# Graph attention and experts on one core: queries from one f32 product in place of three bf16 ones

## The reference, cut to what matters

```python
def _L0_gnn_ref(node_features, edge_index, edge_relations, query_emb, Wq, bq, Wk, ...):
    enh = node_features + 0.1 * query_emb[None, :]
    Q = (enh @ Wq + bq).reshape(N, H, D)
    K = (enh @ Wk + bk).reshape(N, H, D)
    V = (enh @ Wv + bv).reshape(N, H, D)
    src, dst = (edge_index[0], edge_index[1])
    rel = rel_w[edge_relations]
    mod_k = K[src] + 0.2 * rel[:, None, :]
    scores = jnp.einsum('ehd,ehd->eh', Q[dst], mod_k) / D ** 0.5
    seg_max = jax.ops.segment_max(scores, dst, num_segments=N)
    ex = jnp.exp(scores - seg_max[dst])
    denom = jax.ops.segment_sum(ex, dst, num_segments=N)
    w = ex / denom[dst]
    agg = jax.ops.segment_sum(w[:, :, None] * V[src], dst, num_segments=N)
    ...
x = x + _L0_gnn_ref(_layernorm(x), ...)
x = x + _L0_ffn_ref(_layernorm(x)[None], ...)[0]
```

## Time and profile before

| what | us |
|---|---|
| median of three runs | 1356.09 (1348.56 to 1357.88) |
| the profiled execution's own time | 1346.19 |
| its span, first to last instruction | 1344.4 |

### The profile page before, as it was taken

The page is one execution under the profiler, slowest core; times in us unless marked ns, Lnnn a source line. Parts: engine busy times, 40 slices in busy tenths (PEclk is TensorE's granted clock), DMA queues, the critical chain, the costliest instruction groups (busy, mean ns, idle before and its releaser), DMA issues.

```text
span 1344.4 us, 23897 instructions
## 1 busy us (share of the span) xinstructions
PE 1080.3 (80%) x7032; PEld 851.6 (63%) x7033; DVE 894.0 (66%) x1856; ACT 666.2 (50%) x2365; POOL 716.4 (53%) x714
## 2 busy tenths in 40 slices
PE   8978567776767777676677777799599999999997
PEld 3445345555545555555555565567389999999996
DVE  4767767677777877777777768889944444444443
ACT  5532356667667776576676766557511111111111
POOL 4455555555555655555556554756055555445663
PEclk9997777778888978777878878897699999999999
DMA  6266666656766666567666665602744444655332
GB/s 211 94 180 189 195 196 192 202 183 178 221 189 206 193 194 204 179 202 210 198 199 198 174 208 142 202 5 92 256 119 118 100 100 95 184 150 130 53 52 28
DMA packets 112993, 215.77 MB, mean 160 GB/s; under 512 B 19403, under 2 KB 57211, under 8 KB 112891
## 3 DMA queue, kind: packets, MB, share of 16 engines
q0 software_dynamic: 47488, 132.68, 36.7%
q1 hardware_dynamic: 59973, 80.16, 18.4%
q10 hardware_dynamic: 5430, 1.73, 0.6%
HBM read 191.96 MB, written 22.54 MB: 160 GB/s over the span
## 4 chain that ended last, share of the span: by engine, by line
PE 49%; DVE 21%; issue 16%; another core or an unknown queue 9%; ACT 2%; DMA 1%; DVEq 1%; SPq 0%; POOL 0%; POOLq 0%
PE qe_ps L1920 13%; PE bank L1929 8%; PE qe_ps L1732 6%; DVE ring L881 6%; PE bank L1772 5%; PE bank L1920 4%; DVE acc L893 3%; PE qe_ps L1772 2%; DVE ring L875 2%; DVE score L887 2%; PE qe_ps L1837 1%; PE qe_ps L1650 1%; PE qe_ps L1909 1%; PE bank L1650 1%
## 5 line engine op out<-in xcount | busy, mean ns | idle before, releaser
L632 POOL DMA_INDIRECT ring<-kv_table,src_idx x440 | 421.0, 957 | 330.4 <-DVE ring L881 181.5
L1502 ACT ACTIVATE wv<-ring,wgt 128x64 f32<-128x64 f32 x1628 | 407.3, 338 | 52.9 <-remote 46.5
L1732 PE MATMUL qe_ps<-q,hot_t 128*128 x1320 | 237.1, 316 | 140.0 <-issue 87.6
L1732 PEld LDWEIGHTS qe_ps<-q,hot_t 128*128 128x128 bf16 x1320 | 134.6, 110 | 209.0 <-issue 179.3
L1772 PE MATMUL bank<-wv,hotf 128*128 128x260 f32 x588 | 188.6, 451 | 25.2 <-issue 18.8
L697 POOL DMA_INDIRECT out<-room,slot_i x64 | 119.2, 1863 | 154.9 <-DMA out<-room,slot_i 81.4
L1920 PEld LDWEIGHTS qe_ps<-xg_t,ring 128*128 128x128 f32 x1536 | 181.4, 192 | 4.9 <-issue 1.7
L1621 ACT ACTIVATE act<-qe_ps 128x512 f32<-128x512 f32 x64 | 38.2, 597 | 294.7 <-PE bank L1920 140.9
L875 DVE TENSOR_TENSOR ring<-ring,bank 128x1024 f32<-128x1024 f32 x110 | 133.3, 1212 | 75.8 <-remote 63.3
L1920 PE MATMUL qe_ps<-xg_t,ring 128*128 128x128 f32 x1536 | 182.0, 275 | 1.3 <-issue 0.7
L881 DVE TENSOR_TENSOR ring<-ring,qe_ps 128x512 f32<-128x512 f32 x220 | 148.8, 677 | 26.1 <-remote 18.2
(11 more groups left out here) (339 smaller groups left out, 1504.5 us busy)
## 6 DMA issues: line engine op xcount, KB each, us to landing
ring<-in_w SPq DMA_DIRECT2D x48, 512.0 KB, 7.1
t_row<-t_rows SPq DMA_DIRECT2D x55, 256.0 KB
d_row<-d_rows SPq DMA_DIRECT2D x55, 256.0 KB
ring<-kv_table,src_idx POOLq DMA_INDIRECT x440
kv_table<-ring SPq DMA_DIRECT2D x25, 256.0 KB, 2.0
out<-acc SPq DMA_DIRECT2D x26, 128.0 KB, 1.7
x_table<-ring SPq DMA_DIRECT2D x26, 128.0 KB, 1.9
ring<-in_x SPq DMA_DIRECT2D x12, 256.0 KB, 9.0
```

The costliest lines, as they stand in the source:

```text
L632: pool.indirect_dma_start(ring[:, u, place(g) * D:(place(g) + 2) * D], None, kv_table, bass.IndirectOffsetOnAxis(ap=src_idx[:, 4 * g + u:4 ...
L1502: ins = act.activation(wv[:, g % WV_N, u, h, 0:HD], v_rows(g)[:, u, h * HD:(h + 1) * HD], ACT.Copy, scale=w[:, col:col + 1])
L1732: ins = pe.matmul(q_ps[p % AHEAD][:, u * D:(u + 1) * D], hot_t[:, p // 4 % HB_N, hot_cols(p, u)], tile_of(q3, q_tiles[p % 4])[:, k * D:(k ...
```

## The change

Q stays in one f32 tensor `q_all`, copied from PSUM by ACT alone (`keep_q`). The one-hots are f32, six octs of them instead of seven. `queries` does one f32 product per step instead of three bf16 ones. `turn_hot` reads the high halves of the f32 one-hots as bf16. The pieces of Q go, with their semaphores. The tensors that lay over `q3` for the stage behind get their own space (`later`), and x lies over `q_all`. The copy `first` is made one oct earlier.

```diff
-HB_N = 7
+HB_N = 6
-        q3 = sb("q3", [P, NODE_TILES, 3 * D], BF16)
+        q_all = sb("q_all", [P, NODE_TILES, D])
+        later = sb("later", [P, KC * D + 2 * D + KC * NX + NX])
...
-        hot_t = eb("hot_t", [P, HB_N, 8 * P], BF16)
+        hot_t = eb("hot_t", [P, HB_N, 8 * P])
...
-            def rest_of_q(t):
-            def low_piece(t):
-            def pieces_of_q(first, end):
-            def pieces_beside(p):
-            pieces_of_q(0, Q_FIRST)
...
                 if rows_due:
                     factor_rows(rows_due)
-                    v.tensor_copy(first[:, :], hot_t[:, rows_due * CS // 8 % HB_N, 0:1])
+                if maxima_due:
+                    v.tensor_copy(first[:, :], hot_t[:, maxima_due * CS // 8 % HB_N, 0:1])
...
-            def high_piece(t):
+            def keep_q(t):
                 s_q.wait(act, t)
-                act.activation(q3[:, t, 0:D], q_bank(t), ACT.Copy).then_inc(s_high.sem, 1)
-            def middle_piece(t):
-                s_rest.wait(act, t)
-                act.activation(q3[:, t, D:2 * D], rest[:, t % 3, :], ACT.Copy).then_inc(s_mid.sem, 1)
+                act.activation(q_all[:, t, :], q_bank(t), ACT.Copy).then_inc(s_qk.sem, 1)
...
             def project_q(t):
-                s_rest.wait(pe, t - 3)
+                s_qk.wait(pe, t - 3)
...
-                s_lo.wait(pe, min(p, NODE_TILES - 1))
+                s_qk.wait(pe, min(p, NODE_TILES - 1))
                 for u in range(2):
-                    for k in range(3):
-                        ins = pe.matmul(q_ps[p % AHEAD][:, u * D:(u + 1) * D], hot_t[:, p // 4 % HB_N, hot_cols(p, u)], tile_of(q3, q_tiles[p % 4])[:, k * D:(k + 1) * D],
-                                        start=(k == 0), stop=(k == 2))
+                    ins = pe.matmul(q_ps[p % AHEAD][:, u * D:(u + 1) * D], hot_t[:, p // 4 % HB_N, hot_cols(p, u)], tile_of(q_all, q_tiles[p % 4]), start=True, stop=True)
...
-                    ins = pe.transpose(turn_ps.bitcast(BF16)[:, u * P:(u + 1) * P], hot_t[:, o % HB_N, u * P:(u + 1) * P], identb[:, :])
+                    ins = pe.transpose(turn_ps.bitcast(BF16)[:, u * P:(u + 1) * P], hot_t[:, o % HB_N, u * P:(u + 1) * P].bitcast(BF16)[:, 1::2], identb[:, :])
```

More of the change, by code:

```diff
@@ L301, in build @@
         assert at[0] <= NT * H * HB
-        q3_flat = q3[:, :, :].rearrange("p t c -> p (t c)").bitcast(F32)
+        x_again = q_all[:, :, :].rearrange("p t c -> p (t c)")
+        xre = q_all[:, :, :]
         at[0] = 0
[L306 to L313, removed]
+        w_o = carve(later, KC * D).rearrange("p (k n) -> p k n", k=KC)
+        gamma = carve(later, D)
+        beta = carve(later, D)
+        gate_w = carve(later, KC * NX).rearrange("p (k n) -> p k n", k=KC)
+        gate_b = carve(later, NX)
         w_expert = flat[:, 0:WB * WX].rearrange("p (b n) -> p b n", b=WB)
@@ L351, in build @@
         xn_st = late[:, 8 * P:8 * P + 2 * D].rearrange("p (b c) -> p b c", b=2)
-        at[0] = 3 * 4 * P
-        hot_flat = hot_t[:, :, :].rearrange("p m c -> p (m c)").bitcast(F32)
+        at[0] = 3 * 8 * P
+        hot_flat = hot_t[:, :, :].rearrange("p m c -> p (m c)")
         dval = carve(hot_flat, STEPS)
@@ L357, in build @@
         typ = carve(hot_flat, STEPS // 2, BF16)
-        assert at[0] <= HB_N * 4 * P
+        assert at[0] <= HB_N * 8 * P
         dst_t = late[0:PP, 0:4 * P].rearrange("p (q c) -> p q c", q=4)
@@ L371, in build @@
         w_q = [a[:, :, :].rearrange("p i c -> p (i c)") for a in (ends2, wgt)]
-        rest = carve(wv_flat, 3 * D).rearrange("p (s n) -> p s n", s=3)
         dif3 = carve(wv_flat, 3 * NT).rearrange("p (i t) -> p i t", i=3)
@@ L457, in build @@
         s_xn, s_xt, s_enh, s_mm, s_ev, s_kv = (Count(sem(n)) for n in ("s_xn", "s_xt", "s_enh", "s_mm", "s_ev", "s_kv"))
-        s_q, s_high, s_rest, s_mid, s_lo = (Count(sem(n)) for n in ("s_q", "s_high", "s_rest", "s_mid", "s_lo"))
+        s_q, s_qk = (Count(sem(n)) for n in ("s_q", "s_qk"))
         s_kst = [sem(f"s_kst{i}") for i in range(NS)]
@@ L741, in _ @@
                 row_scales(i)
-            def rest_of_q(t):
-                s_high.wait(v, t)
-                s_lo.wait(v, t - 3)
-                v.tensor_tensor(rest[:, t % 3, :], q_bank(t), q3[:, t, 0:D], ALU.subtract).then_inc(s_rest.sem, 1)
-            def low_piece(t):
-                s_mid.wait(v, t)
-                v.tensor_tensor(q3[:, t, 2 * D:3 * D], rest[:, t % 3, :], q3[:, t, D:2 * D], ALU.subtract).then_inc(s_lo.sem, 1)
-            def pieces_of_q(first, end):
[L753 to L756, removed]
             v.wait_ge(s_qe, 32)
@@ L995, in _ @@
                     factor_rows(rows_due)
-                    v.tensor_copy(first[:, :], hot_t[:, rows_due * CS // 8 % HB_N, 0:1])
+                if maxima_due:
+                    v.tensor_copy(first[:, :], hot_t[:, maxima_due * CS // 8 % HB_N, 0:1])
                 if scored:
                     multiply(4 * o)
-                pieces_beside(4 * o)
                 take_sums(o, 0)
@@ L1005, in _ @@
                     type_hot(1)
-                pieces_beside(4 * o + 1)
                 take_sums(o, 1)
@@ L1014, in _ @@
                     multiply(4 * o + 2)
-                pieces_beside(4 * o + 2)
                 take_sums(o, 2)
@@ L1018, in _ @@
                     multiply(4 * o + 3)
-                pieces_beside(4 * o + 3)
                 if o + 2 < BATCHES:
@@ L1470, in steps_links @@
                 ins.then_inc(event("diffs").sem, 1)
[L1472 to L1476, removed]
+            for i in range(NODE_TILES):
+                keep_q(i)
                 if i == Q_FIRST - 1:
-                    middle_piece(i)
                     steps_links()
@@ L1776, in turn_scores @@
                 if ch == 0:
-                    s_rest.wait(pe, NODE_TILES - 1)
+                    s_qk.wait(pe, NODE_TILES - 1)
                 bank_free(("score", ch))
```

## The result

The kernel after takes 1426.95 us (median of 4 runs, 1421.74 to 1429.04). The kernel before, run beside it, takes 1353.9. The ratio is 1.0536, with a 95% interval of 1.0486 to 1.0587: 73 us slower. The profiled execution of after took 1421.74 us, its span is 1420.0.

A forecast was written before the change was run, and what follows sets the result against it. DVE's order was taken to set the pace in most octs, PE where its clock is low or it crawls. 15 + 52 + 14 - 8 = +73 us on 1356 gave 1429 us, range 1350 to 1500.

The forecast's parts named there:

- (b): Six octs: one-hots wait for transposes of the same oct, 49 waits of 1.4 us, three quarters taken: +52 us.
- (a): PE's queries: f32 products dearer than bf16, 29 us at most at the low clock, half taken: +15 us.
- (c): DVE's one-hots in f32: 0.75 us each instead of 0.48: +14 us.
- (d): Pieces of Q gone from DVE in the first six octs, 1.3 us saved per oct: -8 us.
- (e): PE's transposes of the f32 one-hots' high halves: strided weight loads cost no more: 0 us.
- R4: Rival: the strided weight load of the transposes is slow, +49 us, 1478 us; chance 0.08.
- R1: Rival: faster, since PE's crawl goes with its number of instructions and the wait is covered, 1342 us; chance 0.12.
- R2: Rival: the one-hots' wait is covered but f32 is not, +35 us, 1391 us; chance 0.22.
- R3: Rival: the one-hots' wait shows in full, 127 us, in all +162 us, 1518 us; chance 0.13.
- What would show it: Signs in the profile after: dearer f32 queries and one-hots, waits of about 1.4 us in 49 places, octs of 15 us.

The follow-up runs named there:

- e1: The kernel before with six octs of bf16 one-hots instead of seven (and the copy of first an oct earlier): 1407.5 us, 1.0606 of before.
- e9: The kernel after itself, run once more beside the kernel before on another chip: 1417.2 us, 1.0632 of before.
- e10: The kernel after with seven octs of f32 one-hots instead of six, on the same chip as e9: 1341.0 us, 1.0048 of before.
- e6: The kernel after with gathers of only 64 of 128 partitions from the 21st quad on, on the 1165 us chip: 1283.6 us, 1.1023 of before.
- e5: The kernel after with seven octs of f32 one-hots instead of six, on the chip with before at 1165.2 us: 1172.2 us, 1.0047 of before.
- e3: The kernel before with two bf16 query products per step instead of three: 1354.3 us, 1.0224 of before.
- e12: The kernel before with gathers of only 64 of 128 partitions from the 21st quad on: 1350.9 us, 1.0039 of before.
- e4: The kernel after with the transposes in slot 1 of the oct instead of slot 2: 1403.6 us, 1.0564 of before.

## Why the prediction was right

The time was 1427 where 1429 was forecast, and the mechanism (the wait of the one-hots for the transposes of the same oct) is the one that e1 isolates. But the sum is that close by luck, because two errors nearly cancel: the wait cost 24 to 27 us more than was taken for it, the rest 14 to 15 us less. And what ends the long waits is not what was forecast. Step by step:

- **(b), the wait, 52 us taken: measured 76 (e9 against e10) and 79 (e1).** "A wait that falls where PE is late anyway costs nothing twice" holds, but "I take three quarters" of 49 x 1.4 us was off in both factors. Without stand-stills a wait is 2.4 us in the mean (e6), not the 1.4 of one undisturbed oct: 31 of the 49 are 1.3 to 1.9, and 18 are 2.1 to 4.9. The mean lies near the 2.5 of the earlier trace rows, which I kept for the upper end. With stand-stills about two thirds of that price show, 76 of 118 us (two chips, and the 118 with half of the gathers). The step that was wrong is to take one oct for all 49, where those of four successive octs differ by a factor of three. The stand-stills the prediction had seen, but not that the new wait would be stretched by them: 34 of the 49 waits of after are over 5 us and end 1.4 to 4.5 us after the transposes.
- **(a) + (c) + (d), +21 us taken: measured +5.5 and +7.0.** The sizes were right one by one: L1695 has 880 records and 290.7 us (some 290 forecast) for 237 before, the one-hots take 0.753 us in the median (0.75 forecast) and 16.8 us more in all (14 forecast). Yet with seven octs most of this does not show in the time. A half of (a)'s low-clock cost, 15 us, and all of (c), 14, were too much. That they fall into DVE's idle time is argued, not shown, and it is not the whole: on the chip where DVE is 98% busy they cost 7 us too. There the pieces of Q that are gone may pay for the one-hots (DVE is busy 889.8 us in e5, 894.0 in before), which was not separated.
- **(d), -8**: DVE's one-hots of the seventh oct begin at 163.16 us in after and at 168.80 in before, 5.6 us earlier. This includes what (a) and (c) cost in the first octs, so it does not give (d) by itself.
- **(e), 0**: the strided weight loads have a median of 98 ns, the same as a bf16 load of the queries before. R4 falls. The rule of the Trainium skill ("TensorE: Matmul & The Clock Gate", section on weight-path perf modes), by which the fast load stands for column steps up to 1,024 elements, agrees with this trace.
- **R1** (PE's crawl goes with its number of instructions) falls: e3 has 440 products fewer and is slower, and on the chip of e5 the same program as e10 runs without any "remote" wait. The rule of the Trainium skill ("Runtime: NRT & Kernel Launch", Instruction fetch mechanics) that crossing a block of instructions is mostly hidden was not tested by itself; no gain from fewer instructions is seen in e3 or e10, which is in line with it.
- **R2** (the wait covered) falls by e1. **R3** (the wait in full, 127 us) was wrong for the chips with stand-stills, but is close to the 118 us of the chip without.
- **What would show it**: octs of 15 us came (15.1). "Idle time before it that ends with PE L1747, about 1.4 us in 49 places" came in part: 46 places between 160 and 870 us (30 + 14 + 2), but 219.6/46 = 4.8 us each in the mean, and most of it "remote".

No version whose results are the reference's beat before. The best one with the change is that of e5 and e10, half a per cent slower than before.

## What to carry to other kernels

When a buffer loses a place to pay for wider elements, ask first which release the producer waits for now, and whether it is made in the same round of the loop; here the place was worth 76 us and the wider elements and products 6. Price such a wait from all rounds of one period, not from one round: here a period is four octs, and the waits in it run from 1.3 to 4.4 us. And before trading a place away, look for dead memory: the 4 KB that were missing lay in a tensor that is needed only when the buffer is no longer.

## What was not expected of the hardware

- **Two kinds of chip.** The same kernel before took 1328 to 1354 us beside the runs on some chips and 1165 on another, with the granted clock in the loop at 0.82 and, for e5 on the fast one, 0.96. The difference shows as stand-stills: in most octs the engines that wait go on 1.4 to 4.5 us after the instruction that they wait for is recorded as done (3.0 us in the timeline of after above; 4.6 in e1, transposes done at 566.37, the copy on ACT begun at 570.93). In the chain of work that ended last they are a share of their own, 15% in after and none in e5. The chain by engine, after first:

```profile
PE 40%; DVE 26%; another core or an unknown queue 15%; issue 12%; DVEq 2%; ACT 1%; DMA 1%; POOL 1%; ACTq 0%; POOLq 0%; PEldq 0%
```

```profile
PE 43%; POOL 16%; DVE 15%; issue 12%; DMA 7%; ACT 4%; DVEq 1%; POOLq 0%; ACTq 0%; PEldq 0%
```

They don't depend on the bytes that the gathers bring (e12), nor on where the transposes stand (e4). Whether they come with the lower clock, or the clock and the delays have one cause, no run shows.
- **The stand-stills end with a run of gathers.** In the 34 waits of after that are over 5 us, DVE starts 1.6 to 2.1 us after the end of POOL's last gather (median 1.7), however long the transposes have been done; the timeline above has 574.13 and 575.85. In e1, e4 and e9 the medians are 1.6, 1.6 and 1.6 us, while those from the transposes are 3.7, 5.1 and 2.8. In the 15 other octs of after DVE starts while a gather runs or within 0.2 us of its end, and there the signal of the transposes takes 0.1 to 0.4 us. Whether POOL's gathers hold the signals back on these chips is not shown: POOL itself waits for DVE's products, so both can follow DVE's order, and all runs have the same 440 gather instructions. On the chip of e6 the same gathers run, and all 49 waits end within 0.5 us of the transposes.
- **A wait swallows the stand-stills.** Before, they fall at three places of DVE's order; with the new wait nearly all of them fall at it. A view of waits then puts 220 us down to one wait whose removal gives back 76.
- **Fewer products, slower kernel** (e3), at a granted clock of 0.79 for 0.82.
